# Other places in a batch for the keys', values' and turning matmuls of a four-layer attention kernel

## What is computed

```python
def attention(q_in, kv_in, wq, bq, wk, bk, wv, bv, wo, bo):       # 16 heads of 8
    q, k, v = split(q_in @ wq.T + bq), split(kv_in @ wk.T + bk), split(kv_in @ wv.T + bv)
    attn = softmax(mask(q @ k.T / scale), axis=-1)
    return merge(attn @ v) @ wo.T + bo

x = x + attention(_layernorm(x), ctx, ...)          # A0: 256 queries, 512 keys
x = x + _L0_ffn_ref(_layernorm(x), ...)             # F0: quantised gelu network
x = x + attention(_layernorm(x), ctx, ...)          # A1
x = x + _L1_ffn_ref(_layernorm(x), ...)             # F1: 8 experts, 2 chosen, and a shared one
x = x + attention(_layernorm(x), ctx, ..., mask)    # A2: one mask over queries and keys
x = x + _L2_ffn_ref(_layernorm(x), ...)             # AS: causal self-attention (256 keys), F2: 8 gated experts
x = x + attention(ctx, ctx, _layernorm(x), ...)     # A3: a mask over keys
x = x + _L3_ffn_ref(_layernorm(x), ...)             # F3: 8 experts and a layernorm
```

## Time and profile before

| | |
|---|---|
| median of 3 runs | 1807.77 us (1807.18 to 1816.76) |
| the profiled execution | 1806.16 us |
| its span, first to last instruction | 1804.4 us |
| mean granted TensorE clock | 0.971 |
| PE matmul busy | 1697.4 us (94%) |
| PE weight load busy | 1148.1 us (64%) |
| DVE busy | 1120.3 us (62%) |
| ACT busy | 1070.6 us (59%) |
| POOL busy | 638.2 us (35%) |
| chain that ended last | PE 80%, DVE 8%, ACT 6%, issue 4%, POOL 2% |

### The profile page before, as it was taken

The page is one execution under the profiler, slowest core; times in us unless marked ns, Lnnn a source line. Parts: engine busy times, 40 slices in busy tenths (PEclk is TensorE's granted clock), DMA queues, the critical chain, the costliest instruction groups (busy, mean ns, idle before and its releaser), DMA issues.

```text
span 1804.4 us, 38536 instructions
## 1 busy us (share of the span) xinstructions
PE 1697.4 (94%) x14287; PEld 1148.1 (64%) x14322; DVE 1120.3 (62%) x3293; ACT 1070.6 (59%) x2146; POOL 638.2 (35%) x1050
## 2 busy tenths in 40 slices
PE   6999978999999999989999999989998999999998
PEld 3555546555569888854444455568885555589997
DVE  5888858788842332257777666656667888633332
ACT  2888852788874444437777755543335888854443
POOL 4445333344332222213443443323353454222221
PEclk9999978899999999979999999999998999999999
DMA  5444202345300000312423144300031653000000
GB/s 163 127 142 142 75 24 94 127 153 159 97 7 1 1 1 1 94 53 83 121 77 103 42 130 137 99 1 1 1 104 61 184 160 117 22 1 7 7 7 7
DMA packets 114853, 132.35 MB, mean 73 GB/s; under 512 B 14934, under 2 KB 78701, under 8 KB 114669
## 3 DMA queue, kind: packets, MB, share of 16 engines
q1 hardware_dynamic: 114668, 129.90, 23.7%
HBM read 83.45 MB, written 46.40 MB: 72 GB/s over the span
## 4 chain that ended last, share of the span: by engine, by line
PE 80%; DVE 8%; ACT 6%; issue 4%; POOL 2%; DMA 0%; SPq 0%; DVEq 0%; POOLq 0%; ACTq 0%
PE ps_s L1422 16%; PE ps_av L1278 14%; PE ps_s L1235 12%; PE ps_t L1398 10%; PE ps_t L1251 4%; PE ps_s L1398 4%; DVE mx L1711 4%; PE ps_t L1262 3%; ACT prob L986 3%; PE ps_m L1325 2%; PE ps_m L1334 2%; PE ps_m L1319 2%; PE ps_m L1312 1%; PE ps_m L1287 1%; PE ps_m L1347 1%
## 5 line engine op out<-in xcount | busy, mean ns | idle before, releaser
L986 ACT ACTIVATE prob<-ps_t 128x512 f32<-128x512 f32 (+1 forms) x1152 | 617.4, 586 | 206.1 <-PE ps_t L1251 199.4
L1711 DVE TENSOR_REDUCE mx<-ps_s 128x1 f32<-128x512 f32 x752 | 474.4, 683 | 84.9 <-PE ps_s L1235 83.2
L1235 PE MATMUL ps_s<-kst,qst 32*128 32x512 f32 (+2 forms) x1248 | 372.4, 479 | 30.1 <-DVE mx L1711 19.8
L1422 PEld LDWEIGHTS ps_s<-w_ffn,prob 128*128 128x128 f32 x2688 | 317.8, 194 | 10.5 <-issue 3.3
L1422 PE MATMUL ps_s<-w_ffn,prob 128*128 128x128 f32 x2688 | 324.4, 278 | 0.0
L1251 PE MATMUL ps_t<-qmx,kst 32*128 32x256 f32 (+1 forms) x2304 | 312.2, 334 | 4.2 <-ACT prob L986 3.9
L1278 PE MATMUL ps_av<-prob,vaug 128*32 128x256 f32 (+1 forms) x4608 | 307.6, 386 | 3.2 <-ACT avs L1027 3.2
L1235 PEld LDWEIGHTS ps_s<-kst,qst 32*128 32x128 f32 x1248 | 159.3, 188 | 220.7 <-issue 96.5
L1173 ACT ACTIVATE prob<-ps_t,b1c 128x512 f32<-128x512 f32 x204 | 125.5, 686 | 238.6 <-PE ps_t L1398 238.6
L2001 DVE SCALAR_TENSOR_TENSOR acc<-ps_s,comb,acc 128x128 f32<-128x128 f32 x336 | 94.6, 345 | 259.5 <-PE ps_s L1422 259.5
L1251 PEld LDWEIGHTS ps_t<-qmx,kst 32*128 32x128 f32 x2304 | 191.6, 188 | 17.0 <-ACT prob L986 10.2
(11 more groups left out here) (239 smaller groups left out, 2257.1 us busy)
## 6 DMA issues: line engine op xcount, KB each, us to landing
kst<-k_parts SPq DMA_DIRECT2D x128, 256.0 KB, 3.5
qst<-q_parts SPq DMA_DIRECT2D x160, 128.0 KB, 3.7
k_parts<-k_hi SPq DMA_DIRECT2D x64, 256.0 KB, 3.0
q_parts<-q_hi SPq DMA_DIRECT2D x80, 128.0 KB, 2.4
ctxT<-in_ctxT SPq DMA_DIRECT2D x32, 256.0 KB, 2.7
k_parts<-k_lo SPq DMA_DIRECT2D x32, 256.0 KB, 3.2
q_parts<-q_lo SPq DMA_DIRECT2D x40, 128.0 KB, 2.4
w_ffn<-in_F_w SPq DMA_DIRECT2D x18, 256.0 KB, 3.0
```

Of the source, the lines that this page charges most:

```text
L986: nc.scalar.activation(row[:, S * kt:S * kt + w], ps_t[TURN[unit(ph, g, n) % 8]][:, 0:w], ACT.Exp).then_inc(sig["exp_done"], 1)
L1235: pe.matmul(dst, qst[p][strip, g, q * 128:(q + 1) * 128], kst[p][strip, g, 0:nk], start=True, stop=True).then_inc(sig["s_ready"], 1)
L1422: mm = pe.matmul(dst, h[:, c, 128 * q:128 * (q + 1)], w2c, start=(c == 0 and not bias), stop=(c == nc_h - 1))
L1711: dve.tensor_reduce(mx[:, buf, i:i + 1], src, AX.X, ALU.max, negate=True).then_inc(sig["max_done"], 1)
```

## The change

A batch's table now depends on whether its keys go early (`keys_early`: not in AS, not in batch 0, and not in the last batch of A0). In all phases but AS, AVT1 goes from (1, 3, 1) to (2, 0, 0) and ONT from (2, 0, 1) to (2, 2, 0). Where keys are early, V goes from (2, 2, 1) to (1, 0, 0), and K, unless it is one for AS, from (1, 0, 0) to (0, 0, 1), with POOL's split of it going from group 1 to group 0. AS keeps its table. The wait in `read_values` is as it was. Seven lines are added, so line numbers behind them are six or seven higher.

```diff
--- before.py
+++ after.py
@@ -387,11 +387,17 @@
 
             return prob[:, g % 2, HEAD_T[n], :], 2 * (n // HG)
 
-        def slots(ph):
+        def keys_early(ph, bt):
+
+            return ph != "AS" and 0 < bt.b < B - (ph == "A0")
+
+        def slots(ph, nph=None, early=False):
 
             s = {(g, 1, 1): "MT" for g in range(1, NG)} | {(0, 2, 0): "MT"}
-            s |= {(1, 2, 1): "AVT0", (1, 3, 1): "AVT1", (2, 0, 1): "ONT", (2, 2, 1): "V", (2, 3, 1): "O", (3, 0, 0): "XT", (3, 2, 0): "Q"}
-            s[(3, 3, 1) if ph == "AS" else (1, 0, 0)] = "K"
+            s |= {(1, 2, 1): "AVT0", (2, 3, 1): "O", (3, 0, 0): "XT", (3, 2, 0): "Q"}
+            s |= {(1, 3, 1): "AVT1", (2, 0, 1): "ONT"} if ph == "AS" else {(2, 0, 0): "AVT1", (2, 2, 0): "ONT"}
+            s[(1, 0, 0) if early else (2, 2, 1)] = "V"
+            s[(3, 3, 1) if (nph or ph) == "AS" else (0, 0, 1) if early else (1, 0, 0)] = "K"
             return s
 
         def early_slots():
@@ -843,9 +849,10 @@
                             if ppph == "A2":
                                 power(ppph, ppbt, 1, ppbt.b * QT, QT)
                             add_bias(ph, bt)
-                            kph, kbt = next_keys(ph, bt)
-                            if kph and kph != "AS":
-                                split_k(kph, kbt)
+                        kph, kbt = next_keys(ph, bt)
+                        if g == 1 - keys_early(ph, bt) and kph and kph != "AS":
+                            split_k(kph, kbt)
+                        if g == 1:
                             if nph == "A3":
                                 prepare_masks(nbt)
                         if g == 2 and nph:
@@ -1073,7 +1080,7 @@
                     vph, vbt = next_values(ph, bt)
                     kph, kbt = next_keys(ph, bt)
                     pph, pbt = preceding(ph, bt, 1)
-                    table = slots(nph or ph)
+                    table = slots(ph, nph, keys_early(ph, bt))
                     for g in range(NG):
                         nxt = unit_after(ph, bt, last, g, 1)
                         past = group_before(ph, bt, g, 2)
```

## The result

The changed kernel takes 1860.2 us (median of 4 runs, 1851.07 to 1863.18) against 1808.4 us for the kernel before on the same occasion: ratio 1.0272, 95% interval 1.0246 to 1.0298. It is slower, as forecast, but by 52 us and not by 22, and it lies outside the range of 1798 to 1844. The profiled execution took 1859.3 us, with a span of 1857.5 us against 1804.4. Its page: span, busy time of each engine, the clock in 40 slices, and the group of `read_values`.

What follows compares the result with a forecast made beforehand. No engine alone bounds a batch; handovers between PE, DVE and ACT do. Terms of +0.94 us per fully moved batch, with other batches' terms, gave +22 on 1806.2: 1828.3, or 1830 as median; range 1798 to 1844.

Steps and rivals of the forecast that it cites:

- a: Group 0's first quarter: K placed there is partly hidden in the wait for maximum 0; +0.31 us a batch.
- b: Group 1: V in K's old place takes nearly the same time up to the values; +0.03 us a batch.
- POOL's split just doesn't hold `qmx`: POOL in group 0: K's split ends at 398.7, before the addition making `qmx` would start at 398.84; cost 0.
- The next context's load waits for V, which comes earlier: 0: Load of the next batch's context: its wait for V ends earlier, so K's move costs nothing there; 0.
- c: Group 2's first quarter: AVT1 there delays ACT's `avs` read and exponentials, which PE then awaits; +1.0 us a batch.
- d: Group 2's third quarter: shorter ONT replaces V, but the last score still needs maximum 4; -0.4 us a batch.
- The sum at full clock: Whole batch with everything moved: +0.94 us in A1; over the program +22 us.
- the `mrow` term: A3: POOL's split no longer stands with `mrow` ahead of group 2's `qmx`; saves 0.41 us a batch.
- a batch with V only: Batches moving V but not K: three at +1.0 us, A2's two at 0.65; 4.3 us together.
- Batch 7: Last batch of A0, A1 and A3: only the turnings move, nothing leaves group 2; +1.0 us each, 3.0 together.
- a clock under 1.00 in the batches: Sign in the changed profile's attention batches: a granted clock below 1.00 would show the prediction wrong.
- rival 3: Added PE waits throttle the clock: K and V of each batch at half clock, +53 us, 1883 us; chance 0.02.

Runs made afterwards that it cites:

- experiment 1: Changed kernel with a second tensor for group 0's stacked sum in odd batches, so ACT's read waits for an older AVT1: 1813.8 us, ratio 1.0036.
- experiment 6: Changed kernel with the second sum tensor, DVE's AVT1 reading one maximum later, and no early keys in A0's batch 5: 1807.2 us, ratio 0.9974.
- 2: Changed kernel with AVT1 alone back in group 1's last quarter; K, V and ONT stay moved: 1813.3 us, ratio 1.0016.
- 7: Kernel before with only K and POOL's split of it moved early; V, AVT1 and ONT in their old places: 1813.1 us, ratio 1.0019.
- experiment 3: Changed kernel with K, V and POOL's split back in their old places; only AVT1 and ONT moved: 1876.9 us, ratio 1.0380.
- 8: Changed kernel with AVT1 back in its old place and no early keys in A0's batch 5: 1810.5 us, ratio 0.9996.
- 9: Kernel before's order in A0 and each batch 0; elsewhere in A1 to A3 the new order, second sum tensor, later DVE step: 1805.5 us, ratio 0.9968.
- experiment 5: Changed kernel with twelve unused identity matmuls in group 2's second quarter, except in A2 and AS: 1845.9 us, ratio 1.0199.

## Why the prediction was wrong in its size, point by point

**a, K into group 0 (+0.31), and b, V in its place (+0.03): right, a little small.** +0.42 and +0.03 between the same values. POOL's split just doesn't hold `qmx`, as said. The sentence "The next context's load waits for V, which comes earlier: 0" **was wrong**, in one batch. It looked at when the load is issued in a middle batch of A1, and not at what K then has to spare in each phase. In A0's batch SP is late by a list of parameter loads, the context landed 2.7 us before K, and the change takes more than that away. Price: 3 to 5.5 us, in eight of the nine traces of kernels whose keys are early there.

**c, AVT1 into group 2 (+1.0): right, and the mechanism is shown.** The steps from maximum 7 to the values gave 4.36 where the trace has 4.33. With the second tensor, which takes away nothing but ACT's wait, 0.84 of it goes (experiment 1), 0.11 more with DVE's step in its right place (6), and with AVT1 back in its old place 0.95 (2).

**d, ONT in V's place (-0.4): right** (-0.36). That the two can't stand there together (0.55 us of waiting for ACT's copy) I had not seen; the whole change avoids it except in the batches whose keys aren't early.

**The sum at full clock: right.** A1 +0.97 (forecast +0.94), A2 +0.45 (+0.55), A3 +0.57 (+0.53, from the `mrow` term, which experiments 2 and 7 show by itself as -0.40), a batch with V only +0.96 (+1.0). Over the program the table above gives 21.4 where 22 were forecast; 1806.2 + 21.4 is 1828. Batch 7 wasn't as forecast, but it evens out: the sixth distance of A1 and A3 grew by 0.4, that of A0 by 1.6 and not by 1.0, since V stands behind ONT there, as in experiment 3 (V waits 0.47 us for ACT's copy).

**The clock: the step that failed.** The prediction named "a clock under 1.00 in the batches" as what would prove it wrong, and that is what came. The sum had no term for it, and rival 3 carried it with a chance of 0.02, at a price of all or nothing (1883: K and V of every batch at half clock). Neither was what happened. About every second batch of A0, A1 and A3 ran in part at the low level, for 1.3 or 2.6 us more each, and beside them the entry into A1 (+5.7) and three batches of AS (+6.0), whose order nobody had touched. Together it is 32 us in the profiled execution, for a term that the sum had at nothing.
The argument against it was that PE waits some tenths in every group already at 1.00. That shows that the clock held with those waits, not that it would with more. Two things in view said that it doesn't always hold: one of its three runs took 1816.8, 9 us above the others, and its own trace has a fall where A0 ends (columns as in the earlier trace rows):

```profile
230.00:251.00 21.00, 16.66 (x154) 8.92 (x154) 8.97 (x24) 10.95 (x23) 8.28 (x8) 0.81 0.00 1
```

There its last distance took 14.77, and 11.79 at full clock in the kernel after: 3 us in a program that was read as unthrottled in the batches. Later runs of the kernel before reach from 1802 to 1837. A term for falls, with the share seen afterwards (half of the 21 changed batches of A0, A1 and A3 at 1.3 to 2.6: 14 to 27 us), would have brought the full-clock 1828 to between 1842 and 1855.

The Trainium skill (TensorE: Matmul & The Clock Gate, "The HAM clock gate") says that the throttled state is the default and that activity releases it; the prediction held against that rule that no stretch of the attention batches showed it. The stretches at 0.88 and 0.94 above do show the low level there, and K shows both: it takes 1.13 us at full clock and 2.05 in experiment 1's chain. That activity alone decides between them isn't shown: the same 6.09 of 7.00 us were followed by a fall once and not the next time. In "Loop structure matters more than you think" the same page of the Trainium skill names a long DMA wait between matmuls as what makes PE cold, and not waits of any length, as the prediction put it. In A1's batches there is none. These are PE's waits in the one that fell to 0.88 (us in total, times, longest), and they are the same, to the tenth, in the next one at 1.00:

```profile
PE ps_t L1258 <- ACT prob L993: 0.6, 1, 0.6
PE ps_m L1341 <- ACT mturn L1039: 0.3, 1, 0.3
```


**What is shown and what isn't.** Shown: the falls account for the difference between batches of the same instructions. They come with ACT's wait and go without it: of the first five distances of A1 and A3, 9 of 20 fell in the two traces of the changed kernel, and none of 60 in those of experiments 1, 2, 6, 7, 8 and 9. None of 30 fell with twelve products of filler, at two different places. Not shown: a rule for when a batch falls. PE's share of busy time isn't one: A2's batches are at 29.0 of 31.3 us, less than A1's 25.0 of 26.3, and their distances are 31.25 in both traces of the changed kernel. Experiment 3 waits more and falls less. Nor can the 32 us be had back by filler alone: experiment 5's best run is still 1838, since its A0 waits for the context and its AS falls as well.

## What to carry to other kernels

Before moving a reader of a shared buffer later, look at who refills the buffer and what stands behind that refill on its engine: here a 0.66 us turning held ACT's exponentials, and a second small buffer was worth some 44 us, while the whole change with it was worth about 3 (experiment 6). A step moved earlier needs its input earlier in every phase, so read the spare time of its load in the one where the DMA queue is fullest, not in a middle batch. And where a kernel depends on TensorE's full clock in almost every stretch, give each added wait a second price, in batches that run in part at the low level, with a wide range, and size it from stretches of the trace that have fallen already and from the spread of the runs.

## What the runs showed that I had not expected

- The clock falls in batches in which PE never waits longer than 0.6 us at a stretch, and in which of them differs between executions of one kernel (A1's first distance: 27.57 and 26.31). A fall costs 1.3 or 2.6 us in a 26.3 us batch, and nearly all begin at the same place in it.
- Adding work made phases faster: with twelve products more in each of 21 batches, the first five distances of A1 took 131.7 us for 137.6 and 133.7 in the two traces without them. The total was 1846 us for 1846 to 1867 (median 1857.5 of eight runs, on other occasions), which is too close to call it faster. The same twelve in another quarter made it 1876.
- A wait for one load of 256 KB cost 3.1 us and then 2.4 more: PE came out of it at half clock (K at 2.05 us for 1.13).
